# Causal softmax attention with 16 small heads: bfloat16 parts and an immediate exponential scale, a first block that ends with its arithmetic, split parts kept for all four chunks, and row maxima sent head by head

## The chip, the cores and the metric

The program runs on one core of a Trainium2 chip. The time is that of the device for one execution, in microseconds (us), and lower is better. It is the median of several runs. One execution, the profiled one, also left a trace; its span is the time from its first to its last recorded instruction. PE is TensorE (matmuls; PEld its weight loads), DVE VectorE, ACT ScalarE, POOL GpSimd, SP SyncE, which here only issues DMAs. "L793" is line 793 of the kernel.

## The reference, cut to what matters

The whole network is eight stages, each adding to `x` of 2048 tokens by 128: softmax attention (this one), channel mix, gated linear attention, channel mix, retention, experts, lightning attention, experts. The change touches the first stage alone:

```python
x = layernorm(x)                                    # [1, 2048, 128]
qkv = x @ W_qkv
q, k, v = split(qkv, 3)
q, k = _layernorm(q, q_scale), _layernorm(k, k_scale)
q, k, v = (t.reshape(B, S, 16, 8) for t in (q, k, v))
scores = einsum('bshd,bthd->bhst', q / sqrt(8), k)  # float32
scores = where(future, finfo.min, scores)           # causal
attn = softmax(scores)
out = einsum('bhst,bthd->bshd', attn, v).reshape(B, S, 128) @ W_out
```

(The first layer norm stands outside the quoted attention function, in what the whole reference does ahead of it.)

## The kernel before, in words

Names: T = 2048 tokens, in NC = 4 chunks of CH = 512 columns; TPC = 4 tiles of P = 128 tokens in a chunk; H = 16 heads of HD = 8, in NG = 4 groups of GH = 4 heads. All of the attention is in `softmax_attention` (L299 to L847), in two blocks; a block ends when every engine has come to the end of its list.

**Precision.** A score is a product of two float32 rows of 8 numbers. The kernel makes it with 16-bit operands: each of q and k is written as PARTS = 3 addends (`parts`: high, middle, low), and the six largest cross products (`PRODUCTS`) become 6 x 8 = MROW = 48 rows of contraction. Three rows more (`PARTS` again) hold the negative row maximum of q in three addends, against rows of ones in k, so that the matmul gives score minus maximum; KROWS = 51. In the kernel before these 16-bit numbers are float16. As float16 has a small range, q and k are first scaled: `scales()` (L499 to L508, DVE) finds the largest of `|q_scale|` and of `|k_scale|`, makes `spread` = 2048 * scale / maximum, a column for each of q and k, and `exp_scale`, a one-column tile by which the exponential undoes it. The rows of ones hold 2**15 (ONE), and the maxima are divided by it (L703).

**Block 1, the prologue (L367 to L641).** SP loads x in chunks, tables, weights, the two scale vectors in two forms each (`srow`, `scol`, L376 to L379), the constant rows (`extra`, L383) and then the weights of all later stages (L384 to L389). For each chunk: x is normalised (DVE `x_variance`, POOL `x_power`, ACT `x_normalise`), transposed (`turn_x`), multiplied with `qkv` (`project`, L555), taken out of PSUM (`take_qkv`, L602 and L605); q and k are normalised (`qk_variance` L473, POOL `qk_power` L433, `qk_normalise` L482), transposed (`turn_qk`, L566) and split: ACT `take_high` (L615) writes the high part, DVE `take_rest` (L489) the remainder, ACT `take_mid` (L620), DVE `take_low` (L496). Each engine's order is written out by hand (DVE L510 to L537, PE L569 to L582, ACT L622 to L641). `parts` has two buffers (chunk modulo 2), so `take_high` of chunk 2 and 3 waits until chunk 0 and 1 are stored (`stored[c - 2]`, L614).

The split parts must be laid out as 48 rows for each pair of heads. That goes over device memory: `store(c)` (L391, DMAs at L403) issues 12 DMAs, 64 to 192 KB each, 1.5 MB in all; `stack(c)` (L407, DMAs at L411) waits for them and issues four loads of 384 KB into `Qs` and `Ks`. SP does store(0), stack(0), store(1), stack(1) and so on to stack(3), all in block 1, each after `low` of its chunk.

**Block 2, the attention (L644 to L846).** The 16 STEPS are pairs (group g, chunk c) of query columns: chunk 0 for groups 0 and 1, then chunks 1, 2, 3 for these groups, then chunks 3, 2, 1, 0 for groups 2 and 3. A step has 4(c+1) units of 128 keys; a unit has, for each of four heads, one score matmul (L793, `scores`, into one of three PSUM banks, ST = 3), one exponential on ACT (L838, into `probs`), and then one group of value matmuls (L807, `values`, float32, 128x32 tiles of the array, two instructions a head). 160 units, 640 exponentials; in the four units on the diagonal the columns shrink to 512, 384, 256 and 128, and POOL zeroes the future (L695). The sums leave PSUM on ACT (L846) and are turned and divided (`turn values`, L827, L742, L744).

Ahead of that the row maxima of each step are needed: `max` items make the scores a second time, transposed in role (L776, two heads a pair, with the mask matmuls L765 and L766 on the diagonal), and DVE reduces them (L726, 128 x 1024, 32 of them in a step of chunk 3, 320 in all). When a step's maxima are whole, DVE writes `negmax` (L732), POOL splits it in three parts with five chained instructions (L703 to L707), PE turns it (L821, `turn max`), DVE copies it to `mrow` (L738), and SP sends it with four DMAs of 3 KB, one a head (L676), into the maximum rows of `Qs`. The first score matmul of the step waits for all four (`max_set`, one semaphore, L790).

The order of PE, ACT and DVE in block 2 comes from `attention_order` (L207 to L297), a small planner that runs when the program is built. It keeps a model time for each engine (a cost for each item: 0.227 us + 0.00075 us a column for an exponential, columns/500 for the values), and picks among the items that can start the one with the earliest due time: `dve - 0.4` for a maximum product, `act - 1.37` for a score, `act + 0.6 * (...) - 1.7` for values. The three engines follow that one list (`PLAN`).

After block 2, `project_out` and the other stages follow, which the change does not touch.

Of the kernel before, what the change touches and what calls it, by code (L numbers as in the profile page):

```python
# [6 lines left out]
FP16 = mybir.dt.float16  # L7
# [5 lines left out]
T = 2048  # L13
D = 128
# [19 lines left out]
ONE = 2.0 ** 15  # L34
WHOLE = 2.0 ** 11
# [27 lines left out]
def build(nc, io):  # L63
    ctx = ExitStack()
    with ctx:
# [48 lines left out]

        stacks = [nc.dram_tensor(name, [NC, 2, MROW, PAIRS * CH], FP16, kind="Internal").ap() for name in ("q_stack", "k_stack")]

# [90 lines left out]
        def attention_order(STEPS, UNIT, u0, MAXIMA, m0):  # L207
# [16 lines left out]
            while pv < NU or tv < NS:  # L224
                can = {}
                free = slot[slots % 2]
                if given < NM and MAXIMA[given][0] <= tm + 1:
                    can["max"] = (free, dve - 0.4)
# [4 lines left out]
                if su < NU and UNIT[su][0] < len(set_end) and su - pv < 2:  # L233
                    n = GH * su + sj
                    can["scores"] = (max(set_end[UNIT[su][0]], exp_end[n - 3] + 0.06 if n >= 3 else 0.0), act - 1.37)
# [14 lines left out]
                if what == "max":  # L250
# [7 lines left out]
                    if given == m0[k + 1]:  # L258
                        dve += 0.25
                        split_end.append(dve + 1.7)  # L260
                if what == "turn max":
# [3 lines left out]
                    set_end.append(dve + 2.6)  # L265
# [10 lines left out]
                if what == "scores":  # L276
# [5 lines left out]
                    act = start + 0.227 + 0.00075 * (CH - off)  # L282
# [16 lines left out]
        def softmax_attention():  # L299

            QK = PAIRS * T // 2
            Qs, Ks = (arena[:, i * QK:(i + 1) * QK].bitcast(FP16).rearrange("p (n t) -> p n t", n=PAIRS) for i in (0, 1))
            at = 2 * QK
            parts = arena[:, at:at + 3 * 2 * CH].bitcast(FP16).rearrange("p (b s r t) -> p b s r t", b=2, s=2, r=PARTS)
# [9 lines left out]
            with ExitStack() as mem:  # L314
# [6 lines left out]
                mwide = own("mwide", [P, GH, P // GH], FP16)  # L321
                mparts = mwide[:, :, 0:PARTS * TPC].rearrange("p j (r t) -> p j r t", r=PARTS)
                mrow = own("mrow", [P, P], FP16)
                ident16 = own("ident16", [P, P], FP16)
                srow = own("srow", [P, 2, D])
                scol = own("scol", [P, 2])
                smax = own("smax", [P, 2])
                srec = own("srec", [P, 2])
                spread = own("spread", [P, 2])
                exp_scale = own("exp_scale", [P, 1])  # L330
# [25 lines left out]
                scaled = sem("a_scaled")  # L356
# [5 lines left out]
                stacked = [sem(f"a_stacked{c}") for c in range(NC)]  # L362

# [3 lines left out]
                with nc.Block() as block:  # L367
                    @block.sync
                    def _(sp):
# [7 lines left out]
                        for i, name in enumerate(("q_scale", "k_scale")):  # L377
                            sp.dma_start(srow[:, i, :], io[name].rearrange("(a n) -> a n", a=1).to_broadcast([P, D])).then_inc(scales_loaded, 16)
                            sp.dma_start(scol[:, i:i + 1], io[name].rearrange("(n a) -> n a", a=1)).then_inc(scales_loaded, 16)  # L379
                        for i, stack_of in enumerate((Qs, Ks)):  # L380
                            for side in (0, 1):
                                row = 64 * side + MROW
                                sp.dma_start(stack_of[row:row + PARTS].rearrange("r n t -> r (n t)"), io["extra"][i]).then_inc(extra_loaded, 16)  # L383
# [7 lines left out]
                        def store(c):  # L391

                            row = PAIRS * CH
                            for s in (0, 1):
                                r = 0
                                for n in (3, 2, 1):
                                    for side in (0, 1):
                                        half = slice(side * P // 2, (side + 1) * P // 2)
                                        if s == 0:
# [1423 lines left out]
```

## Time and profile before

| | us |
|---|---|
| median of 3 runs | 1348.36 |
| range of the runs | 1346.62 to 1359.75 |
| the profiled execution's own time | 1347.1 |
| its span | 1345.3 |
| PE busy | 985.9 (73%) |
| DVE busy | 904.3 (67%) |
| ACT busy | 563.5 (42%) |
| POOL busy | 404.9 (30%) |

All microseconds of the trace are counted from the start of the span. Busy shares are means over stages with quite different limits, so the attention is read by itself: block 1 lasts from 0 to 98.6 us, block 2 from there to about 558.5 us, and the untouched stages fill the rest. A wait "<-X" in brackets ends with X. The profile's recorded matmul durations contain pipeline latency: two that overlap are both "busy".

### The profile page before, as it was taken

How to read it: one execution, taken by the hardware profiler on the slowest of the kernel's cores; microseconds unless marked ns; L12 is line 12 of the kernel's file. 1: busy time of each engine (PE TensorE's matmuls, PEld its weight loads, DVE VectorE, ACT ScalarE, POOL GpSimd, SP SyncE). 2: the span in 40 equal slices, each digit the busy share in tenths (PEclk: the TensorE clock that was granted, in tenths of full speed). 3: DMA queues.
4: the chain of work that ended last, by engine and by line, in shares of the span. 5: the costliest groups of instructions: out<-in, count | busy, mean ns of one | idle time of the engine just before them, and what ended most of it. 6: DMA issues, size and time to landing. Idle time of an engine off the chain costs nothing. (4 is left out here: it accounts for less than half of the span.)

```text
span 1345.3 us, 17310 instructions
## 1 busy us (share of the span) xinstructions
PE 985.9 (73%) x5802; PEld 498.4 (37%) x5802; DVE 904.3 (67%) x1535; ACT 563.5 (42%) x1042; POOL 404.9 (30%) x495
## 2 busy tenths in 40 slices
PE   4207878898889998768656865379993886449994
PEld 2203222222222332345344322246662445326663
DVE  5508778888888871278987997733336998753335
ACT  4304658687889999431003101123333321203333
POOL 3202111101110111144443443146652443416662
PEclk9657879988999999769967996679996976669997
DMA  4791000000000000322200220101112120101114
GB/s 115 160 189 28 2 2 2 1 1 1 2 1 2 2 2 2 127 77 63 68 10 1 63 70 8 32 26 42 42 40 68 59 62 21 32 12 42 42 42 112
DMA packets 53084, 56.29 MB, mean 42 GB/s; under 512 B 7988, under 2 KB 40380, under 8 KB 52988
## 3 DMA queue, kind: packets, MB, share of 16 engines
q1 hardware_dynamic: 48008, 44.96, 13.1%
q0 software_dynamic: 4992, 10.23, 2.8%
q8 instruction: 50, 0.82, 0.3%
q14 instruction: 34, 0.28, 0.1%
HBM read 38.07 MB, written 16.91 MB: 41 GB/s over the span
## 5 line engine op out<-in xcount | busy, mean ns | idle before, releaser
L838 ACT ACTIVATE arena<-ps,exp_scale 128x512 f32<-128x512 f32 (+3 forms) x640 | 346.7, 627 | 125.3 <-PE ps L793 120.2
L726 DVE TENSOR_REDUCE mpart<-ps 128x2 f32<-128x1024 f32 (+3 forms) x320 | 325.2, 1060 | 101.9 <-PE ps L766 50.2
L793 PE MATMUL ps<-arena 51*128 51x512 f16 (+3 forms) x640 | 182.3, 377 | 36.5 <-DMA arena<-mrow 13.4
L776 PE MATMUL ps<-arena 51*128 51x512 f16 (+3 forms) x640 | 131.8, 384 | 61.1 <-PEq L367 43.9
L1066 POOL TENSOR_TENSOR arena<-arena 128x512 f32<-128x512 f32 x96 | 122.2, 1273 | 165.3 <-DVE arena L1119 165.3
L807 PE MATMUL ps<-arena,w 128*32 128x512 f32 (+3 forms) x1280 | 159.5, 572 | 1.5 <-POOL arena L695 1.5
L695 POOL TENSOR_SCALAR_AFFINE_SELECT arena<-arena 128x512 f32<-128x512 f32 x64 | 40.7, 636 | 325.2 <-ACT arena L838 325.2
L1658 ACT ACTIVATE arena<-ps 128x512 f32<-128x512 f32 x78 | 46.6, 597 | 218.7 <-PE ps L1721 177.1
L1568 DVE COPY arena<-ps 128x128 f32<-128x128 f32 x78 | 22.7, 291 | 155.8 <-PE ps L1711 147.9
L793 PEld LDWEIGHTS ps<-arena 51*128 51x128 f16 x640 | 45.7, 95 | 211.0 <-ACT arena L838 185.6
L1105 DVE TENSOR_TENSOR arena<-arena 128x512 f32<-128x512 f32 x62 | 102.4, 1652 | 11.7 <-ACT arena L1172 4.4
L1623 POOL DMA_INDIRECT results<-arena x78 | 76.8, 984 | 90.4 <-DVE arena L1585 80.1
L1612 POOL DMA_INDIRECT arena<-tokens,arena x78 | 75.7, 971 | 77.0 <-DVE arena L1561 53.8
L1119 DVE TENSOR_TENSOR_SCAN arena<-cst,arena 128x512 f32<-128x512 f32 x64 | 87.4, 1366 | 0.0
L1720 PE MATMUL ps<-w,arena 128*128 x156 | 82.3, 610 | 2.9 <-DVE arena L1568 2.4
L1739 PE MATMUL ps<-w,arena 128*128 x624 | 82.7, 275 | 1.1 <-DVE arena L1585 1.1
L1721 PE MATMUL ps<-w,arena 128*128 x156 | 81.2, 603 | 0.0
L1739 PEld LDWEIGHTS ps<-w,arena 128*128 128x128 f32 x624 | 75.8, 192 | 1.5 <-issue 1.5
L776 PEld LDWEIGHTS ps<-arena 51*128 51x128 f16 x640 | 35.4, 97 | 94.0 <-issue 50.3
L192 ACT COPY xt<-ps 128x512 f32<-128x512 f32 x28 | 16.1, 589 | 126.8 <-PE ps L185 126.8
L185 PE MATMUL ps<-cst,xn 128*128 128x128 f32 x96 | 22.2, 393 | 60.8 <-DVE xn L168 59.0
L1216 PE MATMUL ps<-arena 128*128 128x128 f32 x256 | 43.4, 323 | 27.4 <-POOL arena L1066 27.4
(264 smaller groups left out, 1475.4 us busy)
## 6 DMA issues: line engine op xcount, KB each, us to landing
w<-in_w SPq DMA_DIRECT2D x2, 2048.0 KB, 11.1
arena<-results SPq DMA_DIRECT2D x16, 256.0 KB, 5.0
arena<-g_v SPq DMA_DIRECT2D x15, 256.0 KB
arena<-r_v SPq DMA_DIRECT2D x15, 256.0 KB, 3.6
arena<-l_v SPq DMA_DIRECT2D x15, 256.0 KB, 3.6
arena<-q_stack SPq DMA_DIRECT2D x8, 384.0 KB
arena<-k_stack SPq DMA_DIRECT2D x8, 384.0 KB
tokens<-arena SPq DMA_DIRECT2D x8, 256.0 KB, 2.4
```

Source lines behind the costliest of these rows:

```text
L726: nc.vector.tensor_reduce(out=mpart[:, 2 * pl:2 * pl + 2, t, kc], in_=ps[:, bank:bank + 2, 0:width], axis=AX.X, op=ALU.max).then_inc(ring_ ...
L776: ins = nc.tensor.matmul(ps[:, bank + side, 0:width], rows(Qs, side, 2 * g + pl, (c * TPC + t) * P, (c * TPC + t + 1) * P), rows(Ks, side, ...
L793: nc.tensor.matmul(ps[:, n % ST, off:CH], rows(Ks, j % 2, 2 * g + j // 2, kt * P, (kt + 1) * P), rows(Qs, j % 2, 2 * g + j // 2, c * CH + ...
L807: ins = nc.tensor.matmul(ps[32 * j:32 * j + 32, O, off:CH], vg[kt // (NT // 2)][:, kt % (NT // 2), g * GH + j, :], probs[:, u % 2, j, off: ...
L838: nc.scalar.activation(probs[:, n % 2, j[0], off:CH], ps[:, (GH * n + j[0]) % ST, off:CH], ACT.Exp, scale=exp_scale[:, 0:1]).then_inc(exp_ ...
L1066: nc.gpsimd.tensor_tensor(z[:, n % ZB, :], state[:, n % SB, :], q[:, c % 2, :], ALU.mult).then_inc(z_ready, 1)
L1105: nc.vector.tensor_tensor(upd[:, n % 2, :], v_in, k[:, n // HD % 2, :], ALU.mult).then_inc(upd_ready, 1)
L1119: nc.vector.tensor_tensor_scan(out=state[:, n % SB, :], data0=a, data1=upd[:, n % 2, :], initial=0.0 if c == 0 else state[:, (n - HD) % SB ...
L1623: nc.gpsimd.indirect_dma_start(out=result_rows, out_offset=bass.IndirectOffsetOnAxis(ap=result_row[:, s:s + 1], axis=0), in_=y[:, s % YB, ...
L1720: nc.tensor.matmul(ps[:, i % 2, :], xsT[:, i % 2, :], w1[:, expert[i], :], start=True, stop=True)
L1721: nc.tensor.matmul(ps[:, 2 + i % 2, :], xsT[:, i % 2, :], w3[:, expert[i], :], start=True, stop=True).then_inc(up_ready, 1)
L1739: ins = nc.tensor.matmul(ps[:, 7, 0:D], hidT[:, s % 2, f, :], w2[:, expert[s], f, :], start=f == 0, stop=f == NF - 1)
```

## The change

1. All 16-bit tiles of the attention (`stacks`, `Qs`, `Ks`, `parts`, `mwide`, `mrow`, the identity) are bfloat16. `scales()` and the division of the maxima by ONE go; q and k are multiplied by their own scale column (`scale`, the former `scol`), and the exponential takes the constant 8 ** -0.5 as its scale.
2. `parts` has a buffer for each of the four chunks (two more in `w2`); the wait for `stored[c - 2]` goes. The hand-written orders of block 1 change.
3. SP's list in block 1 ends with `store(1)`; stack(1), store(2), stack(2), store(3), stack(3) and the wait for the later weights move to the head of SP's list in block 2.
4. The maxima have a semaphore for each head, and a score matmul waits for its own head's. Of the first four steps (EARLY = 4) ACT sends them, from its own queue, at the place of `turn max` in the plan; SP sends the others.
5. The planner's constants change.

```diff
-stacks = [nc.dram_tensor(name, [NC, 2, MROW, PAIRS * CH], FP16, ...
+stacks = [nc.dram_tensor(name, [NC, 2, MROW, PAIRS * CH], BF16, ...
 # attention_order
-                    can["max"] = (free, dve - 0.4)
+                    can["max"] = (free, dve - 0.62)
-                    can["scores"] = (max(...), act - 1.37)
+                    can["scores"] = (max(...), act - 0.87)
-                    at = exp_end[GH * pv + GH - 1] + (1.2 if UNIT[pv][1] >= STEPS[k][1] * TPC else 0.06)
+                    at = exp_end[GH * pv + GH - 1] + (1.0 if UNIT[pv][1] >= STEPS[k][1] * TPC else 0.06)
-                    can["values"] = (at, act + 0.6 * (GH * (pv + 2) - len(exp_end)) - 1.7)
+                    can["values"] = (at, act + 0.52 * (GH * (pv + 2) - len(exp_end)) - 1.2)
-                        split_end.append(dve + 1.7)
+                        split_end.append(dve + 1.9)
-                    set_end.append(dve + 2.6)
+                    set_end.append(dve + 3.0)
-                    act = start + 0.227 + 0.00075 * (CH - off)
+                    act = start + 0.137 + 0.00075 * (CH - off)
-                    pe += (CH - off) / 500 + 0.02
+                    pe += (CH - off) / 470 + 0.02
 # buffers
-            parts = arena[:, at:at + 3 * 2 * CH].bitcast(FP16).rearrange("p (b s r t) -> p b s r t", b=2, s=2, r=PARTS)
+            room = [arena[:, at + i * 3 * CH:at + (i + 1) * 3 * CH] for i in (0, 1)]
+            room += [w2[:].rearrange("p e f d -> p (e f d)")[:, i * 3 * CH:(i + 1) * 3 * CH] for i in (0, 1)]
+            parts = [r.bitcast(BF16).rearrange("p (s r t) -> p s r t", s=2, r=PARTS) for r in room]
 # block 1, SP
-                            sp.dma_start(srow[:, i, :], io[name]...to_broadcast([P, D])).then_inc(scales_loaded, 16)
-                            sp.dma_start(scol[:, i:i + 1], ...).then_inc(scales_loaded, 16)
+                            sp.dma_start(scale[:, i:i + 1], ...).then_inc(scales_loaded, 16)
-                        for c in range(NC):
+                        for c in (0, 1):
                             sp.wait_ge(low, 2 * (c + 1))
-                            store(c)
-                            stack(c)
-                        sp.wait_ge(loaded, 16 * LOADS)
+                            store(sp, c)
+                            if c == 0:
+                                stack(sp, c)
 # block 1, DVE order
-                        scales()
                         qk_variance(0)
+                        qk_normalise(0)
                         qk_variance(1)
-                        qk_normalise(0)
-                        qk_variance(2)
-                        qk_normalise(1)
-                        dve.wait_ge(scaled, 1)
+                        dve.wait_ge(scales_loaded, 32)
                         take_rest(0)
                         take_low(0)
+                        qk_normalise(1)
+                        qk_variance(2)
                         qk_variance(3)
-                        qk_normalise(2)
                         take_rest(1)
                         take_low(1)
+                        qk_normalise(2)
                         qk_normalise(3)
 # block 1, PE order
                         turn_x(3)
+                        project(3)
                         turn_qk(1)
-                        project(3)
 # block 1, ACT
-                                if c >= 2:
-                                    act.wait_ge(stored[c - 2], 16 * 12)
-                                nc.scalar.mul(parts[:, c % 2, s, 0, :], ps[:, 6 + s, :], spread[:, s:s + 1]).then_inc(high, 1)
+                                nc.scalar.mul(parts[c][:, s, 0, :], ps[:, 6 + s, :], scale[:, s:s + 1]).then_inc(high, 1)
                         take_high(0)
+                        take_mid(0)
                         take_qkv(2)
                         take_x(3)
-                        take_mid(0)
+                        take_qkv(3)
                         take_high(1)
-                        take_qkv(3)
                         take_mid(1)
 # block 2
+                EARLY = 4
+                def set_maxima(eng, k):
+                    g, c = STEPS[k]
+                    eng.wait_ge(ring_read, RING["turn max", k] + 1)
+                    for j in range(GH):
+                        row = 64 * (j % 2) + MROW
+                        eng.dma_start(Qs[row:row + PARTS, 2 * g + j // 2, c * CH:(c + 1) * CH],
+                                      mrow[j * P // GH:j * P // GH + PARTS * TPC, :]).then_inc(max_set[j], 16)
 # block 2, SP
+                        stack(sp, 1)
+                        for c in (2, 3):
+                            store(sp, c)
+                            stack(sp, c)
+                        for k in range(EARLY, NS):
+                            set_maxima(sp, k)
+                        for j in range(GH):
+                            sp.wait_ge(max_set[j], 16 * NS)
+                        sp.wait_ge(loaded, 16 * LOADS)
 # block 2, POOL
-                            link(nc.gpsimd.tensor_scalar(m, m, 1.0 / ONE, None, ALU.mult))
 # block 2, PE
-                            if kt == 0 and j == 0:
-                                pe.wait_ge(max_set, 16 * GH * (k + 1))
+                            if kt == 0:
+                                pe.wait_ge(max_set[j], 16 * (k + 1))
 # block 2, ACT
-                                                     ACT.Exp, scale=exp_scale[:, 0:1]).then_inc(exp_done, 1)
+                                                     ACT.Exp, scale=float(HD) ** -0.5).then_inc(exp_done, 1)
+                            if what == "turn max" and n < EARLY:
+                                set_maxima(act, n)
```

The bodies of `store` and `stack` are as before, with `parts[c][half, s, ...]` for `parts[half, c % 2, s, ...]` and the engine as an argument. The constant rows (`extra`) are the bit patterns of two bfloat16 ones in a float32.

## Rows read from the trace of the kernel before

**Rows 1.** Busy time by stage: us, PE, PEld, DVE, ACT, POOL, clock, DMA share, GB/s.
```profile
0.00:45.50 45.50, 21.35 (x64) 12.77 (x64) 28.09 (x144) 20.54 (x44) 14.01 (x23) 0.89 0.48 120
45.50:98.60 53.10, 3.88 (x16) 3.14 (x16) 11.85 (x19) 6.29 (x10) 5.04 (x3) 0.50 0.91 185
98.60:114.30 15.70, 9.64 (x105) 4.89 (x106) 13.71 (x20) 0.00 (x0) 1.11 (x5) 0.50 0.58 78
114.30:271.40 157.10, 130.73 (x1008) 41.17 (x1003) 125.82 (x141) 104.22 (x199) 21.67 (x54) 0.84 0.01 2
271.40:398.90 127.50, 114.96 (x881) 32.92 (x880) 104.81 (x107) 110.04 (x196) 10.77 (x27) 0.94 0.01 1
398.90:558.50 159.60, 142.56 (x1168) 45.34 (x1164) 94.99 (x118) 139.93 (x263) 24.25 (x58) 0.94 0.01 2
```

**Rows 2.** Timeline of block 1 and its end: start us, us, engine, line, operation.
```profile
22.20 2.13 DVE L482 TENSOR_SCALAR w<-w,qsmall 128x128 f32<-128x128 f32 x8
...
28.88 0.43 SPq L389 DMA_DIRECT2D vec<-in_beta  x1
...
36.61 3.95 SPq L403 DMA_DIRECT2D q_stack<-arena  x6
...
45.95 0.64 SPq L411 DMA_DIRECT2D arena<-q_stack  x1
...
48.61 3.89 SPq L403 DMA_DIRECT2D q_stack<-arena  x6
...
62.11 1.26 ACT L615 ACTIVATE arena<-ps,spread 128x512 f16<-128x512 f32 x2 [8.18 <-DMA k_stack<-arena]
...
78.97 0.58 SPq L411 DMA_DIRECT2D arena<-q_stack  x1
...
95.39 0.58 SPq L411 DMA_DIRECT2D arena<-q_stack  x1
...
98.64 0.29 PE L776 MATMUL ps<-arena 51*128 51x128 f16 x2 [43.93 <-PEq L367]
```

**Rows 3.** Groups by shape, ACT, the whole span: busy us, mean ns, idle before.
```profile
L838 ACT ACTIVATE arena<-ps,exp_scale 128x512 f32<-128x512 f32 x448 | 273.0, 690 | 107.0 <-PE ps L793 102.0
L1658 ACT ACTIVATE arena<-ps 128x512 f32<-128x512 f32 x78 | 46.6, 597 | 218.7 <-PE ps L1721 177.1 <-issue 41.7
```

**Rows 4.** Timeline of one unit late in the attention.
```profile
520.98 1.26 ACT L838 ACTIVATE arena<-ps,exp_scale 128x512 f32<-128x512 f32 x2
...
521.72 0.39 PE L793 MATMUL ps<-arena 51*128 51x512 f16 x1 [0.36 <-ACT arena L838]
...
522.04 1.07 PE L807 MATMUL ps<-arena,w 128*32 128x512 f32 x8
...
522.71 1.44 ACT L838 ACTIVATE arena<-ps,exp_scale 128x512 f32<-128x512 f32 x2
...
523.04 0.81 PE L793 MATMUL ps<-arena 51*128 51x512 f16 x3
```

**Rows 5.** Timeline around the passage between two steps of chunk 3.
```profile
305.76 0.22 DVE L732 TENSOR_REDUCE negmax<-mpart 128x16 f32<-128x64 f32 x1
...
309.42 0.21 DVE L738 COPY mrow<-ps 128x128 f16<-128x128 f16 x1
309.49 1.14 ACT L838 ACTIVATE arena<-ps,exp_scale 128x128 f32<-128x128 f32 x4 [0.44 <-PE ps L793]
...
309.70 2.92 SPq L676 DMA_DIRECT2D arena<-mrow  x4
...
313.74 0.60 PE L793 MATMUL ps<-arena 51*128 51x512 f16 x3 [1.48 <-DMA arena<-mrow]
...
390.32 0.22 DVE L732 TENSOR_REDUCE negmax<-mpart 128x16 f32<-128x64 f32 x1
```

**Rows 6.** Timeline: DVE reduces four full maximum products back to back.
```profile
376.61 4.59 DVE L726 TENSOR_REDUCE mpart<-ps 128x2 f32<-128x1024 f32 x4 [0.38 <-PE ps L776]
```

**Rows 7.** Timeline, first use of chunk 1 in block 2.
```profile
112.25 0.61 PE L776 MATMUL ps<-arena 51*128 51x512 f16 x2 [0.51 <-DVE mpart L726]
```

More of the change, by code:

```diff
@@ L362, in softmax_attention, with store, stack @@
                 stacked = [sem(f"a_stacked{c}") for c in range(NC)]
+                def store(sp, c):
+                    row = PAIRS * CH
+                    for s in (0, 1):
+                        r = 0
+                        for n in (3, 2, 1):
+                            for side in (0, 1):
+                                half = slice(side * P // 2, (side + 1) * P // 2)
+                                if s == 0:
+                                    src = parts[c][half, s, 0:n, :]
+                                else:
+                                    src = parts[c][half, s, 3 - n:4 - n, :].to_broadcast([P // 2, n, CH])
+                                sp.dma_start(bass.AP(tensor=stacks[s].tensor, offset=((c * 2 + side) * MROW + r * HD) * row,
+                                                     ap=[[CH, P // 2], [HD * row, n], [1, CH]]), src).then_inc(stored[c], 16)
+                            r += n
+                def stack(sp, c):
+                    sp.wait_ge(stored[c], 16 * 12)
+                    for side in (0, 1):
+                        for dst, src in ((Qs, stacks[0]), (Ks, stacks[1])):
+                            sp.dma_start(dst[64 * side:64 * side + MROW, :, c * CH:(c + 1) * CH],
+                                         src[c, side].rearrange("r (n t) -> r n t", n=PAIRS)).then_inc(stacked[c], 16)
                 def small_x(i, c):
@@ L488, in take_rest @@
                                 dve.wait_ge(high, 2 * c + s + 1)
-                                nc.vector.scalar_tensor_tensor(out=rest[:, c % 2, s, :], in0=ps[:, 6 + s, :], scalar=spread[:, s:s + 1],
-                                                               in1=parts[:, c % 2, s, 0, :], op0=ALU.mult,
+                                nc.vector.scalar_tensor_tensor(out=rest[:, c % 2, s, :], in0=ps[:, 6 + s, :], scalar=scale[:, s:s + 1],
+                                                               in1=parts[c][:, s, 0, :], op0=ALU.mult,
                                                                op1=ALU.subtract).then_inc(rest_ready, 1)
@@ L619, in take_mid @@
                                 act.wait_ge(rest_ready, 2 * c + s + 1)
-                                nc.scalar.copy(parts[:, c % 2, s, 1, :], rest[:, c % 2, s, :]).then_inc(mid, 1)
+                                nc.scalar.copy(parts[c][:, s, 1, :], rest[:, c % 2, s, :]).then_inc(mid, 1)
                         x_normalise(0)
@@ L658, in softmax_attention @@
                 max_split = sem("a_max_split")
-                max_set = sem("a_max_set")
+                max_set = [sem(f"a_max_set{j}") for j in range(GH)]
+                EARLY = 4
                 st_ready = sem("a_st_ready")
@@ L1797 @@
     order = np.concatenate([turned, D + turned, np.arange(2 * D, 3 * D)])
-    extra = np.zeros((2, PARTS, PAIRS * T), np.float16)
-    extra[1] = ONE
+    extra = np.zeros((2, PARTS, PAIRS * T // 2), np.float32)
+    extra[1] = np.full(1, 0x3F803F80, np.uint32).view(np.float32)
     given = {
```

82 lines of the change are left out of this document (18 added, 64 removed).

## The prediction

> **What bounds the kernel now.** I read the busy time by stage first [rows 1]. The attention takes 558.5 us of 1345.3, in three parts. From 0 to 45.5 us block 1 computes. From 45.5 to 98.6 it hardly does: PE is busy 3.9 us of 53.1 and DVE 11.9, while the DMA engines are busy 0.91 of the time. From 98.6 on the attention proper runs, and the DMA engines are idle.
>
> The timeline of block 1 shows why [rows 2]. SP is one list: it stores a chunk, waits for that, loads it back, and only then goes to the next. Chunk 0 is stored from 36.61 and loaded from 45.95; the loads of chunks 2 and 3 start at 78.97 and 95.39, a period of 16.4 us. ACT could have split chunk 2 from about 54, but waited 8.18 us for a free buffer, until 62.11. PE's next matmul is at 98.64, although it needs chunk 0 alone, loaded long ago. The end of the block is what it waits for.
>
> In the attention proper no single engine is full. From 271.4 to 398.9 ACT's records cover 110.0 us of 127.5 (0.86), PE's 0.90, DVE's 0.82 [rows 1]. One unit shows the reason [rows 4]: the exponential begun at 520.98 ends at about 521.67 (0.69 us, [rows 3]); that frees the third bank, and a score starts at 521.72. At 522.04 the values start and hold PE for 1.00 us; the next score starts at 523.04. ACT's two exponentials from 522.71 last 1.44 us together, so the second begins 0.75 after the first, at 523.46, where two from 520.98 are only 0.57 apart (1.26 - 0.69). So the unit is a closed loop: exponential 0.69, release 0.05, score to values 0.32, values 1.00, score to exponential 0.42: 2.48 us, for four exponentials that ACT could start in 4 x 0.57 = 2.28.
>
> Last, the passage between two steps [rows 5]. The maxima are whole at 305.76, in the row tile at 309.42, sent by 312.62 in four DMAs (2.92 us to issue), and the step's first score starts at 313.74, having waited 1.48 us for them. ACT's last exponential of the old step ended at 310.63. Two such steps take 390.32 - 305.76 = 84.56, 42.3 us each.
>
> **The change, part by part.**
>
> *Prologue.* Arithmetic no longer waits for stores, and the block ends after store(1). First SP. It issues two loads fewer (about 0.45 to 0.85 us each), so the last weight load, now ended at 29.3 [rows 2], ends at about 28. `low(0)` came at 36.5, because `qk_normalise(0)` stood behind `qk_variance(1)` (22.20 [rows 2]) and `take_mid(0)` behind two other ACT items. In the new order I put normalise(0) at 19 to 21.3, high(0) at 22.7, rest, mid and low to 27. So store(0) starts at 28 and, by the 9.3 us of before (36.61 to 45.95), stack(0) at 37.4. Four loads of 0.65 later, store(1) starts at 40.1 and its 12 issues of 0.65 end at 48. The arithmetic: projection of chunk 3 follows that of chunk 2 at once, low(1) comes at 39, chunks 2 and 3 add about 5 us each; `low(3)` at 49 to 51. DVE's load bounds this from below: 28.1 + 11.9 us busy [rows 1] less 1.5 for `scales()`, 38.5. Both lists end near 50, and the first matmul follows at about 51 instead of 98.6: **-47.6**.
>
> What is late next is the DMA. The data movement is the same, at 16.4 us a chunk when nothing else stops it. With stack(0) at 37.4, stack(1) is issued at 53.5, stack(2) at 70, stack(3) at 86.5. A stack needs some 11 us to land: after the one of 95.39 the DMA engines are busy for another 0.58 x 15.7 = 9.1 us of block 2 [rows 1], to about 107. Chunk 0 is there at 49, chunk 1 at about 65. Block 2 first uses chunk 1 13.6 us after its start (112.25 [rows 7]), which would be 64.6: a wait of 0 to 2 us, I take 1. Chunks 2 and 3 are needed some 57 and 100 us after the start and are there. Prologue in all **-46.6**; ends -40 (arithmetic to 55, chunk 1 late by 3) and -51.
>
> *Exponentials.* The trace has the same instruction shape with a constant scale: 597 ns on ACT from PSUM (L1658) against 690 [rows 3], 93 ns less; L1658 is another function, which is the uncertainty. ACT's pure load falls by 640 x 0.093 = 59.5 us. But in the loop above the exponential's duration stands once in four: the unit goes from 2.48 to 2.39, not to 4 x 0.48 = 1.92. Over 160 units, fewer full ones (a step of chunk c has 4c+1; 112 in all), this is 112 x 0.09 = 10 us and about 3 more on the diagonals. The planner's order could break the loop only by filling banks before the values; with three banks and 1.00 + 0.32 + 0.42 us of blockade against three exponentials of 0.48, it can't.
>
> The Trainium skill (ScalarE: Activation LUTs, on speed) says that each per-partition pointer operand adds about 93 ns to an ACTIVATE, and that back-to-back ones overlap by as much. The trace agrees with both, 690 against 597 and 0.57 apart at 0.69. By that rule alone, with ACT as the bound, the whole 59.5 us would come off; the loop through PE is what speaks against it.
>
> *Maxima.* A score waits for its own head's DMA. The first of the four is issued 2.2 us before the last (2.92 less one of 0.70), and POOL's chain is one link of about 0.3 shorter: 2.5 us from the first score of a step where it is exposed. DVE needs 1.12 us a full reduction (three intervals in 4.59 less 1.22, [rows 6]); a step of chunk 3 has 24 full ones and 8 diagonal ones, 34 us. So DVE, at 34 of 42.3, follows the list, and a later planner due time for scores with an earlier one for maxima can draw it nearer to 34.
>
> Sums. Steps of chunk 3, from 271.4 to 398.9: 13 full units x 0.09 = 1.2, and 2.5 of the 3.5 us gap between 310.63 and the new step's first exponential: 3.7 each, three times: **-11**. From 398.9 to 558.5 the maxima are ready in advance (DVE 0.60 busy): 43 full units, 3.9 us, and diagonals: **-6**. From 114.3 to 271.4 the maxima of ever larger steps pace it: ACT is busy 104.2 of 157.1, DVE 125.8, 0.80 [rows 1]. With earlier maxima and shorter passages I take DVE to 0.90, 125.8 / 0.90 = 139.8: -17.3.
>
> *Against it.* For steps 0 to 3 ACT issues the four DMAs itself. The trace has no DMA from ACT. SP's row gives 2.92 us for four [rows 5]; below, nothing if ACT is idle then anyway. ACT waits for DVE's copy first, and all exponentials behind it in the list wait too, then PE for banks. Step 0 finds ACT idle, the others partly: 3 us for steps 1 and 3, none for 2, less what a gap hides: +5, ends 0 and +12. The first two or three sendings also meet full DMA engines; before, the gap from sending to score had none: 0 to 3 us each, within those ends. Early part **-12**, ends +5 and -25.
>
> Bfloat16 for float16 moves the same bytes through the same instructions: nothing. The untouched 786.8 us: nothing.
>
> Sum: -46.6 - 12 - 11 - 6 = -75.6. From the profiled execution's own 1347.1 that gives **1271.5 us** (1.3 below the median of the runs, within their spread).
>
> **Rivals.**
> *ACT's full saving arrives* (the new order keeps PE out of ACT's way): 1347.1 - 46.6 - 59.5 = 1241. For it: ACT is the engine most covered from 398.9 on where it counts, 139.9 of 159.6, the passages between steps included [rows 1]. Against: the 0.75 us interval, in every unit. Chance 0.12. The skill's rule of the pointer operand, above, is the one that leads here.
> *The overlap is paid for*: maxima sent from ACT into full DMA engines, chunk 1 late, and PE at 1.2 GHz (clock 0.50 in [rows 1] from 45.5 to 114.3) for longer. Then the early part costs +5 to +12 where I have -12, and the prologue gives -40: 1347.1 - 40 + 8 - 17 = 1298. Chance 0.17.
> *Hidden anyway*: the first scores wait for chunk 3's data in some way I overlook, so the prologue gives nothing; 1347.1 - 29 = 1318. PE's wait at 98.64 is for the block, and chunk-by-chunk semaphores are in the code, so 0.04.
> *Slower*: the planner's later due time for scores. If in each unit that also carries maxima (steps 0 to 8, 96 units) the score behind the values is queued after a maximum product that waits for DVE's bank, ACT loses one reduction, 1.12 us [rows 6], a unit: +107 us, 1347.1 - 46.6 - 6 + 107 = 1401. It decides from (46.6 + 6) / 96 = 0.55 us a unit. Against: the planner models exactly this wait. Chance 0.03.
> My forecast: 0.64.
>
> **How the numbers follow.** The two late terms, -17 together, can be -7 (shorter passages bring nothing) or -26 (DVE and ACT closer packed). The forecast's ends together are 1347.1 - 51 - 22 - 26 = 1248 and 1347.1 - 40 - 1 - 10 = 1296; the range of the same width leaves out about 2 in 10, mostly 1241, 1298 and beyond. About 1% is what a measurement can tell here: faster by over 1% 0.95 (the forecast, the first two rivals and half of the third), within 1% 0.02 (its other half, should the attention gain nothing either), slower by over 1% 0.03.
>
> **What would show it.** Block 2's first matmul at 49 to 53; SP's L411-type loads in block 2; no 8 us wait of ACT on a store. The exponential's mean at 0.60 with 0.48 between neighbours, yet a full unit at 2.35 to 2.45 us in the steps without maxima: if it is under 2.2, the loop was wrong. First score 2.5 us earlier after the row copy. DMA issues on ACT at four places, near 0.7 each. DVE over 0.88 covered in the steps of chunk 3. A block 2 longer than 445 us would say that the new order or ACT's sending costs more than I give; one of under 415 that the loop did not hold.

## The result, and the profile after

The changed kernel takes 1300.19 us (median of 4 runs, 1295.03 to 1301.77) against 1353.86 for the one before in the same comparison: a ratio of 0.960, 95% interval 0.953 to 0.967. The kernel before takes about 1348 or about 1358 us from run to run (of ten runs on one chip, six took 1347.1 to 1348.5 us at a mean granted clock of 0.838 to 0.842, four 1357.6 to 1359.2 at 0.828 or 0.829), its median of 1353.86 lies between the two, and what decides between them no run shows. The profiled execution of the changed kernel took 1301.57, span 1299.8. I had said 1271.5 and a range up to 1296. Counted as the forecast was, from the profiled execution's 1347.1, the gain is 45.5 us, not 76.

The same view as [rows 1], of the kernel after, with the stages cut at the same events (block 2's first matmul, the first exponential of step 0, of step 6, of step 9, the end of block 2; the last row is one spell inside the last stage):

```profile
0.00:51.90 51.90, 22.97 (x80) 14.33 (x80) 40.54 (x156) 26.30 (x53) 18.58 (x25) 0.83 0.68 147
51.90:69.70 17.80, 9.65 (x101) 4.75 (x101) 14.13 (x20) 0.00 (x0) 0.83 (x4) 0.50 0.95 209
69.70:230.70 161.00, 136.41 (x1007) 42.60 (x1006) 125.66 (x141) 88.29 (x198) 20.00 (x48) 0.79 0.17 33
230.70:347.10 116.40, 112.47 (x870) 32.19 (x870) 104.13 (x104) 92.78 (x195) 9.83 (x24) 0.96 0.01 1
347.10:514.30 167.20, 152.27 (x1180) 46.35 (x1176) 94.62 (x119) 118.53 (x264) 22.72 (x52) 0.88 0.01 2
471.50:498.80 27.30, 25.68 (x110) 4.54 (x109) 0.85 (x4) 15.60 (x36) 3.80 (x6) 0.50 0.00 1
```

| stage | before | after | difference | forecast |
|---|---|---|---|---|
| block 1 | 98.6 | 51.9 | -46.7 | -46.6 |
| to the first exponential | 15.7 | 17.8 | +2.1 | -12 with the next |
| steps 0 to 5 | 157.1 | 161.0 | +3.9 | |
| steps 6 to 8 | 127.5 | 116.4 | -11.1 | -11 |
| steps 9 to 15 | 159.6 | 167.2 | +7.6 | -6 |
| the rest | 786.8 | 785.5 | -1.3 | 0 |

So two terms came out to the tenth, and two have the wrong sign. In the late stage ACT does its work in 118.5 us instead of 139.9 and PE covers 152.3 instead of 142.6: what ACT saved is more than spent again. Block 2 lasts 514.3 - 51.9 = 462.4 us, above the 445 at which the prediction said that the new order or ACT's sending costs more than it gave.

The exponential's group by shape after [rows 3]: 606 ns for 690, 84 less (I had 93, from L1649's former self, L1658).

```profile
L827 ACT ACTIVATE arena<-ps 128x512 f32<-128x512 f32 x448 | 234.0, 606 | 123.5 <-PE ps L782 123.4
L1649 ACT ACTIVATE arena<-ps 128x512 f32<-128x512 f32 x78 | 46.6, 597 | 218.9 <-PE ps L1712 218.9
```

A full unit of the kernel after, at full clock:

```profile
330.99 2.06 ACT L827 ACTIVATE arena<-ps 128x512 f32<-128x512 f32 x4 [0.33 <-PE ps L782]
...
331.64 0.39 PE L782 MATMUL ps<-arena 51*128 51x512 bf16 x1
...
331.96 1.07 PE L796 MATMUL ps<-arena,w 128*32 128x512 f32 x8
...
332.96 0.39 PE L782 MATMUL ps<-arena 51*128 51x512 bf16 x1
```

The next unit's first exponential starts at 333.38, 2.39 us after this one's at 330.99. It is the median of the full units from step 9 on, where the kernel before has 2.48.

The end of block 1 and the start of block 2, timeline of the kernel after [rows 2, 7]:

```profile
28.98 3.99 SPq L369 DMA_DIRECT2D q_stack<-arena  x6
...
38.38 0.64 SPq L377 DMA_DIRECT2D arena<-q_stack  x1
...
51.94 0.29 PE L765 MATMUL ps<-arena 51*128 51x128 bf16 x2 [3.20 <-PEq L383]
...
54.76 0.58 SPq L377 DMA_DIRECT2D arena<-q_stack  x1
...
62.77 3.90 ACTq L653 DMA_DIRECT2D arena<-mrow  x4
...
67.46 0.61 PE L765 MATMUL ps<-arena 51*128 51x512 bf16 x2 [2.40 <-DMA arena<-k_stack]
...
75.15 0.22 DVE L727 COPY mrow<-ps 128x128 bf16<-128x128 bf16 x1 [1.67 <-PE ps L810]
...
75.40 3.06 ACTq L653 DMA_DIRECT2D arena<-mrow  x4
...
78.57 2.22 ACT L827 ACTIVATE arena<-ps 128x256 f32<-128x256 f32 x8 [4.94 <-issue]
...
84.76 1.21 PE L782 MATMUL ps<-arena 51*128 51x512 bf16 x3 [2.74 <-DMA arena<-mrow]
```

Each of my times for block 1 is within 1.3 us: store(0) at 28.98, stack(0) at 38.38, stack(1) at 54.76, first matmul at 51.94. Chunk 1 was 2.40 us late, not 1. What follows is what I had priced too low. ACT issues step 1's maxima from 75.40 to 78.46 and starts no exponential in between; 4.94 us of its time go, waiting for the row copy (75.15) included. And the DMA issued at 75.40 lets the first score go only at 84.76, 9.4 us later; in [rows 5], with idle DMA engines, it was 4.0 us from the first issue although all four were waited for.

### The profile page after: what moved, and what is told of

It is laid out like the page before. It is cut to its first block and busy times, and to the rows that moved or that the text cites. A ratio compares the mean times of both kernels' runs of the same rounds, so it can differ in the third digit from the quotient of the medians.

```text
span 1299.8 us, 17329 instructions
## 1 busy us (share of the span) xinstructions
PE 994.5 (77%) x5802; PEld 497.3 (38%) x5802; DVE 903.7 (70%) x1529; ACT 508.2 (39%) x1042; POOL 400.1 (31%) x479
## 5 line engine op out<-in xcount | busy, mean ns | idle before, releaser
L827 ACT ACTIVATE arena<-ps 128x512 f32<-128x512 f32 (+3 forms) x640 | 292.5, 541 | 155.1 <-PE ps L782 145.7
L782 PE MATMUL ps<-arena 51*128 51x512 bf16 (+3 forms) x640 | 187.5, 386 | 17.0 <-ACT arena L827 8.8
L796 PE MATMUL ps<-arena,w 128*32 128x512 f32 (+3 forms) x1280 | 168.9, 603 | 4.6 <-ACT arena L827 3.7
L765 PE MATMUL ps<-arena 51*128 51x512 bf16 (+3 forms) x640 | 152.0, 388 | 23.3 <-DVE mpart L714 15.3
L1649 ACT ACTIVATE arena<-ps 128x512 f32<-128x512 f32 x78 | 46.6, 597 | 218.9 <-PE ps L1712 218.9
L782 PEld LDWEIGHTS ps<-arena 51*128 51x128 bf16 x640 | 50.3, 96 | 186.7 <-ACT arena L827 146.4
L1603 POOL DMA_INDIRECT arena<-tokens,arena x78 | 75.7, 970 | 76.9 <-DVE arena L1552 53.7
L765 PEld LDWEIGHTS ps<-arena 51*128 51x128 bf16 x640 | 37.5, 97 | 69.3 <-DVE mpart L714 47.2
```

The lines of the kernel that those rows point to most:

```text
L765: ins = nc.tensor.matmul(ps[:, bank + side, 0:width], rows(Qs, side, 2 * g + pl, (c * TPC + t) * P, (c * TPC + t + 1) * P), rows(Ks, side, ...
L782: nc.tensor.matmul(ps[:, n % ST, off:CH], rows(Ks, j % 2, 2 * g + j // 2, kt * P, (kt + 1) * P), rows(Qs, j % 2, 2 * g + j // 2, c * CH + ...
L796: ins = nc.tensor.matmul(ps[32 * j:32 * j + 32, O, off:CH], vg[kt // (NT // 2)][:, kt % (NT // 2), g * GH + j, :], probs[:, u % 2, j, off: ...
L827: nc.scalar.activation(probs[:, n % 2, j[0], off:CH], ps[:, (GH * n + j[0]) % ST, off:CH], ACT.Exp, scale=float(HD) ** -0.5).then_inc(exp_ ...
```

## The experiments

A table of all runs first. "To exp 0" is from block 2's first matmul; the other columns run from first exponential to first exponential of the steps named, the last one to the end of the last exponential. Low: the us within that last stretch at a granted clock of 0.50, that is at 1.2 GHz, summed from the clock records of the trace. Spell: the longest stretch at 0.50 that began in it (it can run on beyond its end; that of e8_before_newplan began 0.3 us ahead of it). All columns but the first come from one profiled execution each. e11_after_again is the changed kernel once more and repeats them within 0.3 us.

| run | median us | to exp 0 | 0-2 | 2-4 | 4-6 | 6-9 | 9-end | low | spell |
|---|---|---|---|---|---|---|---|---|---|
| before | 1348.4 | 15.7 | 27.0 | 55.4 | 74.6 | 127.5 | 155.6 | 15.6 | 17.1 |
| after | 1300.2 | 17.8 | 36.1 | 53.4 | 71.5 | 116.4 | 163.9 | 37.5 | 27.3 |
| e1_plan_back | 1294.9 | 18.2 | 32.5 | 55.2 | 70.9 | 118.8 | 157.8 | 36.7 | 27.3 |
| e2_pointer | 1305.2 (one) | 16.4 | 34.7 | 54.0 | 72.6 | 119.5 | 165.8 | 27.3 | 6.8 |
| e3_serial_act | 1324.6 (one) | 14.7 | 31.5 | 53.2 | 73.6 | 116.6 | 154.5 | 10.2 | 3.4 |
| e4_serial_sp | 1317.6 (one) | 14.7 | 27.2 | 47.3 | 72.0 | 116.6 | 160.3 | 27.3 | 6.8 |
| e5_early2 | 1283.6 | 17.7 | 32.6 | 50.3 | 68.8 | 119.1 | 158.2 | 36.7 | 27.3 |
| e6_filler | 1277.5 | 18.0 | 32.7 | 50.1 | 69.4 | 119.7 | 148.7 | 3.4 | 3.4 |
| e7_pool | 1283.8 | 18.7 | 33.4 | 50.4 | 69.0 | 119.3 | 157.4 | 35.8 | 30.7 |
| e8_before_newplan | 1357.9 (one) | 15.7 | 30.0 | 53.6 | 75.7 | 126.2 | 168.9 | 37.2 | 10.2 |
| e9_maxima_first | 1278.9 | 14.7 | 30.8 | 49.0 | 69.9 | 119.5 | 149.4 | 9.7 | 13.7 |
| e10_first_filler | 1278.0 | 15.5 | 30.4 | 49.0 | 69.9 | 119.5 | 147.5 | 0.0 | none |
| e11_after_again | 1301.4 | 17.8 | 36.3 | 53.3 | 71.5 | 116.3 | 163.9 | 37.5 | 27.3 |

**The planner's order.** My theory after reading the result: the order, not the exponentials, spoils the late steps. In the trace after, the second unit of steps 8, 9 and 11 (first exponential to that of the third unit) takes 5.9, 5.1 and 6.6 us; before it was 2.5 to 3.1. The timeline after, step 8:

```profile
309.10 0.88 PE L782 MATMUL ps<-arena 51*128 51x512 bf16 x2
310.08 0.39 PE L765 MATMUL ps<-arena 51*128 51x512 bf16 x2
311.30 1.08 PE L816 MATMUL ps<-cst,arena 128*128 128x128 f32 x4 [0.83 <-DVE mpart L714]
312.31 1.94 PE L796 MATMUL ps<-arena,w 128*32 128x512 f32 x8
...
314.18 0.51 PE L782 MATMUL ps<-arena 51*128 51x512 bf16 x1
...
314.79 1.58 ACT L827 ACTIVATE arena<-ps 128x512 f32<-128x512 f32 x3 [3.79 <-PE ps L782]
```

PE's list there is: scores with three maximum products among them, the turn of a finished step's values (L816), then the values (L796). The turn needs a slot of the two that DVE empties, and these were just filled with maxima: PE stands until 311.30, the values are right behind, PE is at 1.2 GHz (granted clock 0.50 from 311.1 to 314.5; 1.94 us for the values, not 1.07), and ACT waits 3.79 us. The planner's function, run with either set of constants, shows where it comes from: the new list puts the turn of steps 6, 7, 9 and 10 off by a whole step, until it stands right before the first values of steps 8, 9, 11 and 12, which may not come ahead of it. In step 12, where two scores stand between the last maximum product and the turn, the second unit stays at 3.1 us. In the list of before, scores stand between each of these turns and the next values.

`e1_plan_back`:

```diff
-  can["max"] = (free, dve - 0.62)       -  can["scores"] = (..., act - 0.87)
+  can["max"] = (free, dve - 0.4)        +  can["scores"] = (..., act - 1.37)
   (and the six other constants of attention_order as before)
```

> The changed kernel with all the planner's constants of before, the rest unchanged. Theory (the new order of PE is at fault late in the attention): the second unit of steps 8 to 13, 2.9 to 6.6 us in the changed kernel, goes back to 2.5 to 2.8, the 27 us at 1.2 GHz from 471.5 us vanish, the full unit stays 2.39, and the stretch from the first exponential of step 9 to the last exponential, 163.9 us, shrinks to about 150; whole kernel about 1286 us. Rival (the shorter exponentials by themselves leave PE too idle and let its clock fall): that stretch stays at 160 or more with a long spell at 1.2 GHz, and the kernel stays at 1297 to 1303.

A turn in step 8 in its timeline, with the scores between it and the values:

```profile
313.35 0.63 PE L816 MATMUL ps<-cst,arena 128*128 128x128 f32 x4 [0.47 <-DVE mpart L714]
313.91 0.39 PE L782 MATMUL ps<-arena 51*128 51x512 bf16 x2
314.23 1.06 PE L796 MATMUL ps<-arena,w 128*32 128x512 f32 x8
```

The second units are 2.6 to 3.0 us again in steps 8 to 12 (3.4 in step 13, which runs into the spell), and from step 9 on the seven second units sum to 21.5 us instead of 28.5. But the 27 us at 1.2 GHz stayed, so the stretch is 157.8, not 150, and the kernel 1294.9, not 1286 (one of its four runs took 1286.8, at a mean clock of 0.853 where the others have 0.839 to 0.842). The theory explains the second units, not the spell. The new constants did buy something: steps 6 to 8 are 2.4 us longer without them.

`e8_before_newplan` is the mirror image: the kernel before, all eight constants new.

> The kernel before with the planner's new constants alone. Theory (the new order puts the turn of the values behind a full ring of maximum products and the next values right behind it): the second unit of steps 8, 9 and 11 takes 4 to 6 us and not 2.5 to 3.1, the stretch from the first exponential of step 9 to the last one is 3 to 8 us longer than 155.6, while the steps of chunk 3 (127.5 us from step 6 to step 9) get no longer. Rival (the new order only hurts together with the shorter exponentials): second units as before.

As the theory says for the units: second ones of 6.3, 5.5 and 6.5 us in steps 8, 9 and 11, with the old exponentials too, and steps 6 to 8 at 126.2. From step 9 on it takes 168.9 us, +13.3, more than the 3 to 8 that I gave it. The order is not all of that: the stretch also has 37.2 us at 1.2 GHz where the kernel before has 15.6, and by the price of such time found below (0.34 us each) that is about 7 of the 13 us. Its one total, 1357.9, lies within the range of the kernel before in the same comparison (1345.8 to 1358.2) and shows nothing.

**The exponential.** `e2_pointer`:

```diff
-  ACT.Exp, scale=float(HD) ** -0.5)
+  ACT.Exp, scale=exp_scale[:, 0:1])     # a column that holds 8 ** -0.5
```

> The changed kernel with the exponential's scale read from a one-column tile (same value) and not as a constant. Both theories: an exponential of 512 columns goes from about 600 to 690 ns and the full unit from 2.39 to 2.48 us, so 112 full units cost 10 us. Theory (order): the long second units remain, kernel 1310. Rival (shorter exponentials let the clock fall): the spell at 1.2 GHz late in the attention goes, and the kernel is no slower than 1300.

```profile
L829 ACT ACTIVATE arena<-ps,exp_scale 128x512 f32<-128x512 f32 x448 | 272.8, 691 | 83.8 <-PE ps L784 79.2
```

691 ns again, and the full unit, 2.39 us in the kernel after, is 2.48 in this one: the loop of the prediction. The long spell is absent and the second units stay long. The total of one run is 1305, between the two forecasts. But the next two runs have the short exponential, the new order and no long spell either, and e8_before_newplan has the long exponential and 37.2 us at 1.2 GHz, so a shorter exponential does not bring the low clock by itself.

The Trainium skill (ScalarE: Activation LUTs, on speed) puts a pointer operand at about 93 ns an instruction; the two runs show 691 against 606, 85. That is a price of the instruction alone: of the 0.34 us that four exponentials save, the full unit got 0.09.

**Load and ACT's issuing.** `e3_serial_act` puts the DMAs back into block 1, `e4_serial_sp` has EARLY = 0 besides:

```diff
 # block 1, SP
-  for c in (0, 1): ... store(sp, c); if c == 0: stack(sp, c)
+  for c in range(NC): ... store(sp, c); stack(sp, c)
 # block 2, SP: stack(1), store(2), stack(2), store(3), stack(3) removed
```

> The changed kernel with all stores and stacks in block 1 again (block 2 starts near 93 us and finds idle DMA engines), maxima of steps 0 to 3 still sent by ACT. Theory (load on the DMA engines is what costs early): from block 2's first matmul to the first exponential 15 us, not 17.8; from the first exponential to that of step 2 about 28 us, not 36.1; the kernel about 1300 + 41 - 11 = 1330. Rival (ACT's own issuing costs it): the 36.1 us stay at 33 or more, kernel about 1338.

> As the run before it, but SP sends the maxima of all steps (EARLY = 0). The difference to it is the price of ACT's issuing alone: I expect 3 to 8 us less from the first exponential of step 0 to that of step 4. If ACT's issuing is hidden, no difference (within 2 us).

From the first exponential of step 0 to that of step 4, busy times as above, first of e3_serial_act, then of e4_serial_sp:

```profile
104.90:189.50 84.60, 70.55 (x534) 23.36 (x534) 64.48 (x77) 42.14 (x101) 13.36 (x32) 0.76 0.01 2
```

```profile
102.60:177.10 74.50, 63.24 (x536) 22.11 (x533) 64.36 (x77) 42.14 (x101) 13.32 (x32) 0.87 0.01 2
```

ACT and DVE do the same work to a tenth of a microsecond, in 84.6 us with ACT's issuing and 74.5 without, at a granted clock of 0.76 against 0.87. So four sendings by ACT cost 10.1 us there (11.8 up to step 6), above my 3 to 8. By step it is 2.8, 1.5, 3.6 and 2.3 us: most of the 4 x 3 us of issuing is not hidden. What part of the 10.1 is the lower clock, which came with it, no run separates. The load is the difference between the kernel after and e3_serial_act: 3.1 us to the first exponential (2.4 of them the wait for chunk 1), 4.6 in steps 0 and 1, 5.9 in all up to step 6. Each of the two rival explanations holds for its part. e3_serial_act as a whole came out 5 us below the lower of my two totals, since the serial block 1 was faster than assumed (block 2 from 90.2, and from 88.0 in e4_serial_sp).

These two runs and the kernel after also have the same list and the same exponentials from step 9 on. That stretch in e3_serial_act, e4_serial_sp and the kernel after (columns as in the first fence, the clock third from the end):

```profile
379.70:534.30 154.60, 139.50 (x1160) 44.94 (x1156) 94.32 (x118) 117.85 (x263) 22.17 (x51) 0.97 0.01 2
```

```profile
365.60:525.90 160.30, 145.71 (x1160) 45.54 (x1156) 94.28 (x118) 118.05 (x263) 22.09 (x51) 0.91 0.01 2
```

```profile
347.10:510.90 163.80, 150.09 (x1160) 45.26 (x1156) 94.40 (x118) 117.89 (x263) 22.09 (x51) 0.89 0.01 2
```

The same work takes 154.5, 160.3 and 163.9 us with 10.2, 27.3 and 37.5 us of it at 1.2 GHz: 0.34 us more for each microsecond at the lower clock, whether in one spell or in several (e4_serial_sp has none above 6.8). A unit says the same: 3.69 us in the spell against 2.39 loses 1 - 2.39 / 3.69 = 0.35 of the time. And e2_pointer and e4_serial_sp both have 27.3 us at 1.2 GHz and the new list: 165.8 - 160.3 = 5.5 us is what the shorter exponential is worth late, where I had 6.

`e5_early2`: e1_plan_back with EARLY = 2.

> The changed kernel with the planner's constants of before and with EARLY = 2: ACT sends the maxima of steps 0 and 1 alone, SP those of steps 2 and 3 (it has issued its last stack by 91 us, before the row copy of step 2 at about 100). ACT's issuing in steps 2 and 3 goes. Theory (ACT's issuing is not hidden, 10 us for four steps): from the first exponential of step 2 to that of step 4 about 50 us, not 55.2, whole kernel 4 to 6 us below the run with the planner's old constants alone. If only steps 0 and 1 pay, no difference.

From step 2 to step 4 50.3 us against 55.2, as expected; the kernel takes 1283.6 us (0.949 of before, 0.943 to 0.955). The profiled executions are 6.1 us apart, the medians 11.3, more than the 4 to 6 expected. SP was free for these two steps: its last stack is issued by 91.2 us, step 2's row copy comes at 98.8.

`e7_pool` moves the two sendings that are left to POOL, with semaphores of their own:

```diff
-  if what == "turn max" and n < EARLY: set_maxima(act, n)      # ACT
+  if i < EARLY: set_maxima(pool, i)                            # POOL, behind split_maxima(i)
```

> As the run with EARLY = 2, but POOL and not ACT sends the maxima of steps 0 and 1, behind its split of them. Theory (ACT's issuing blocks the exponentials): from the first exponential to that of step 2 about 28 us, not 32.5, if a DMA from POOL is as quick as one from ACT. Rival (the DMA engines' load delays the sending whoever issues it): 32 us or more, and possibly later, as POOL must also cut the diagonal units' future.

The rival is right: 33.4 us for steps 0 and 1. Four issues take POOL 2.19 us, ACT is not blocked, and the score still starts at 85.12:

```profile
75.12 0.22 DVE L733 COPY mrow<-ps 128x128 bf16<-128x128 bf16 x1 [0.92 <-PE ps L816]
...
75.64 2.19 POOL L657 DMA_DIRECT2D arena<-mrow  x4 [1.78 <-DVE mrow L733]
...
85.12 0.80 PE L788 MATMUL ps<-arena 51*128 51x512 bf16 x2 [2.73 <-DMA arena<-mrow]
```

Whoever issues it, a 3 KB DMA beside a stack takes 9 us from issue to score here. With the load on, taking the issuing off ACT wins nothing (33.4 us against 32.6); without the load it does, in steps 0 and 1 too (31.5 against 27.2). The two prices overlap.

The Trainium skill (DMA: Bandwidth & Descriptors, on queues) says that a DMA engine takes the queues for which it has work in turn, packet by packet. From that I would have inferred that a small DMA on a queue of its own need not wait for another's backlog, and stays near the 4.0 us of the idle case. The runs, 9.4 from ACT and 9.5 from POOL, say that a separate queue is no cure here. Where in its way the small DMA spends the 5 us more no run shows.

`e9_maxima_first` therefore makes room instead:

```diff
 # block 2, SP, with EARLY = 0 and the planner's old constants
   stack(sp, 1)
+  set_maxima(sp, 0); set_maxima(sp, 1)
   store(sp, 2); stack(sp, 2)
+  set_maxima(sp, 2)
   store(sp, 3); stack(sp, 3)
```

> The changed kernel with the planner's constants of before, no sending by ACT (EARLY = 0), and this list for SP in block 2: stack(1), maxima of steps 0 and 1, store(2), stack(2), maxima of step 2, store(3), stack(3), maxima of the rest. So the DMA engines are idle while step 1's maxima go out. Theory (load on the DMA engines delays the sending of steps 0 and 1, whoever issues it): from the row copy of step 1 to its first exponential 3 to 5 us, not 10; from the first exponential to that of step 2 27 to 29 us, not 32.5; kernel 1275 to 1281. Rival (chunk 2 then comes late, or step 2's maxima wait behind its loads): what is won there is lost again before step 4, kernel 1284 or more.

Row copy to first exponential of step 1 is 4.2 us (10.3 in the kernel after), and the first exponential of all comes 14.7 us into block 2. Step 2's maxima now wait behind the loads of chunk 2: 8.4 us, so the 30.8 us of steps 0 and 1 missed the 27 to 29, and the rival has its share. The kernel takes 1278.9 us: 0.946 of before (0.941 to 0.951).

**The spell.** `e6_filler` (on e5_early2) and `e10_first_filler` (on e9_maxima_first) add to PE's list:

```diff
+  if what == "scores" and j[0] == 2 and at_plan > last_max:
+      nc.tensor.matmul(ps[:, 5, :], rows(Ks, 0, 0, 0, P), rows(Qs, 0, 0, 0, CH), start=True, stop=True)
```

> As the run before it, and once the last maxima are out PE makes one more 51x512 product after the third score of each unit, into a PSUM bank that nobody reads; its result is left out of everything. Theory (PE falls to 1.2 GHz late in the attention because it has too little to do, and stays there because values at 1.2 GHz stretch the unit to 3.7 us): no spell of more than 7 us at 1.2 GHz in steps 12 to 15, the stretch from the first exponential of step 9 to the last one 147 to 150 us in every run, and a smaller spread of the times. Rival (the fall has another cause): the long spell shows again, or the extra product costs about 0.2 us a unit and 18 units make it 4 us slower.

> As the run before it, with the extra 51x512 product on PE after the third score of each unit once all maxima are out (result unused). Theory: the late spell at 1.2 GHz is gone, and the median is 5 to 10 us below that run, near 1270. Rival (the spell comes from elsewhere): median within 3 us of it.

In both profiles the late spell is gone and steps 9 to 15 take 148.7 and 147.5 us, with 3.4 and 0.0 us of them at 1.2 GHz. The medians say less: 6.1 us under e5_early2, but 0.9 under e9_maxima_first instead of the 5 to 10 expected, where the profile had 9.7 us at 1.2 GHz to lose. The smaller spread of the times didn't come either: one run of each filled kernel took 1292, at a mean granted clock of 0.843 and 0.846 where its others have 0.859 to 0.864. Those two left no trace, so where their time went is not known. The extra product is inconclusive as a remedy.

`e11_after_again`, the changed kernel on the chip of the last two:

> The changed kernel itself once more, beside the two runs above on the same chip: 1295 to 1302 us, with a long spell at 1.2 GHz late in the attention in the slower of its runs; what it shows is how far the two versions lie below it.

1301.4 us (0.962 of before, 0.956 to 0.967), all four runs at a clock of 0.839 to 0.844, and in the profile the same 27.3 us spell. e9_maxima_first is 22.5 us faster than it on the same chip, and beats both kernels.

## Why the prediction was wrong

*Block 1* was right in its chain and nearly in its size. That -46.7 stands beside -46.6 is luck in the last us: my term was -47.6 for the block and +1 for chunk 1, and they came out at -46.7 and +2.4.

*The loop through PE* was right: 2.48 to 2.39 us a full unit, with the pointer operand as the control. The rival that the whole ACT saving arrives is out. (The overlap of neighbouring exponentials, for which I had called the 93 ns of the Trainium skill (ScalarE: Activation LUTs, on speed) confirmed, is 0.12 us in the row itself, 0.69 - 0.57; no term hangs on it.) *Steps 6 to 8*, -11.1 for -11, had the right mechanisms and some luck. The three gaps from one step's last exponential to the next one's first sum to 3.4 us instead of 9.3, 6.0 less where I had 7.5 (from the row copy to the first exponential 3.8 to 4.0 us instead of 4.8 to 5.0, where I had 2.5 less), and 2.4 of the 11.1 go back with the planner's old constants (e1_plan_back), which I had not priced.

*The early part* was mis-sized in three terms: -12 forecast, +6.0 measured. First, ACT's issuing: I wrote +5 with an end of +12, on the argument that ACT is partly idle then anyway; it is 11.8 without load, some lower clock included. An engine that issues DMAs in order holds back not its own idle time but everything that waits for its next result, PE's list and through it DVE's. Second, the load: I gave the first sendings 0 to 3 us and put them inside the same ends; it is 5.9 on top, the wait for chunk 1 included. Third, the step "I take DVE to 0.90": DVE was busy 125.7 of 161.0, 0.78. Without load and ACT's issuing (e4_serial_sp) it comes to 0.86, and the part measures 161.1 us against 172.7, -11.6, where my -17.3 stood. 6.8, 5.9 and 5.7: the 18 us that are missing.

*The late part*, -6 forecast, +8.3 measured from first exponential to last. The failed step is "From 398.9 to 558.5 the maxima are ready in advance": I took the order of PE's list as given and PE's clock as before, and priced only durations, though I had named the planner's due times as a rival and looked for their harm in the wrong place, in every unit instead of at the turn of the values, once a step. The exponentials' part held, 5.5 us (e2_pointer against e4_serial_sp) for 6. With the old constants and little low clock (e9_maxima_first) the stretch takes 149.4. Of the 14.5 us from there to the kernel after, the list is 5.1 (154.5 in e3_serial_act against 149.4, both with about 10 us at 1.2 GHz), most of it in the second units, and 27 us more at 1.2 GHz are 9.4 (163.9 against 154.5). e8_before_newplan shows the list's part from the other side. Why the clock is low for 10 us in one profile and 37 in another stays open: with the new list it is 10.2, 27.3 and 37.5, with the old one 9.7, 35.8 and 36.7, and each figure is one execution.

The range failed on the upper side because two parts left their ends: +6.0 early, where the worst was +5, and -11.1 + 7.6 = -3.5 for the two late stages, where it was -7. The rival at 1298 had the right mechanism for the early part (+5 to +12), and at 0.17 too small a chance. That its total comes near the measured one is luck all the same: it gave 7 us too few to the prologue and missed the late part as I did.

## What to carry to other kernels

When a planner's costs are changed, read the list that comes out, above all at the places that come once a step: an item that waits for a ring slot must not stand right before the item on which the next engine depends. Price a DMA that a computing engine issues at its full issue time on everything that waits for that engine, and ask what else is on the DMA engines at that time; moving it to another queue doesn't help, moving the large transfers behind it does. Moving transfers out of a barrier's way is worth nearly all that it promises, and the bill comes in the first steps. And before two orders of work are compared, compare how long each profile ran at 1.2 GHz: here that alone was worth 9 us between executions that did the same work.

## What the runs showed of the hardware

PE can stay at 1.2 GHz for long while its records look full. In the spell from 471.5 to 498.8 they cover 25.7 of 27.3 us (the last row of the first fence): the values take 1.93 us instead of 1.07, ACT waits for its scores, and the unit takes 3.69 us instead of 2.39.

```profile
477.42 2.07 ACT L827 ACTIVATE arena<-ps 128x512 f32<-128x512 f32 x4 [1.19 <-PE ps L782]
...
478.61 1.93 PE L796 MATMUL ps<-arena,w 128*32 128x512 f32 x8
...
481.12 2.07 ACT L827 ACTIVATE arena<-ps 128x512 f32<-128x512 f32 x4 [1.63 <-PE ps L782]
```

With one more 512-column product per unit, two profiles show 3.4 and 0.0 us at 1.2 GHz from step 9 on. Four DMAs of 3 KB take ACT 3.0 to 3.9 us to issue, in which it starts no exponential; from the first issue to the score that waits took 4.0 us with idle DMA engines and 9.4 to 9.5 beside large transfers.
